# Causal attention in chunks of query blocks i and 7-i instead of 512 neighbouring queries, with one clip a step

## What is computed

```
Q = concatenate([Qc, Qr], axis=-1)          # (4, 16, 2048, 24)
K = concatenate([Kc, Kr], axis=-1)
scores = clip(einsum('bhqd,bhkd->bhqk', Q, K), -80.0, 80.0)
scores = where(causal, scores, -inf)
weights = softmax(scores / sqrt(24), axis=-1)
attn = einsum('bhqk,bhkd->bhqd', weights, V)
return attn.transpose(0, 2, 1, 3).reshape(B, S, 256) @ W_O
```

## Time and profile before

| | |
|---|---|
| runs | 2262.58, 2269.71, 2274.1 us; median 2269.71 us |
| profiled execution | 2265.95 us, of which the span is 2264.2 us |
| attention stage in the span | about 1093 to 2178 us |
| busy over the span | PE 2013.3 us (89%), DVE 1710.7 (76%), ACT 1582.6 (70%), POOL 829.8 (37%) |
| instructions | 45005 |
| instruction fetches by DMA | queue q8 149 packets, 2.44 MB; queue q14 53 packets, 0.43 MB |
| granted TensorE clock, mean | 0.968 |

### The profile page before, as it was taken

One profiled execution on the slowest core, in us unless ns is written; L12 is line 12 of the kernel. 1 busy time (PEld: TensorE's weight loads), 2 busy tenths in 40 slices (PEclk: granted clock), 3 DMA queues, 4 the chain that ended last, 5 costly groups with the idle time before them and its releaser, 6 DMA issues. The chain is left out here.

```text
span 2264.2 us, 45005 instructions
## 1 busy us (share of the span) xinstructions
PE 2013.3 (89%) x18726; PEld 906.9 (40%) x18726; DVE 1710.7 (76%) x2493; ACT 1582.6 (70%) x1833; POOL 829.8 (37%) x653
## 2 busy tenths in 40 slices
PE   5999999999995878788799989989999989999985
PEld 2656556556563554555222222222222222222243
DVE  7866676675748899998577788777788777788874
ACT  5545455464544554555799999989999989999951
POOL 1645445455365666766111111111111111111135
PEclk9999999999996999989899999999999999999997
DMA  3001001001112555547421233330333330233337
GB/s 97 19 19 32 26 20 38 19 20 38 48 38 84 164 159 153 168 130 195 116 49 41 68 76 72 75 71 20 76 76 76 71 74 16 67 76 81 112 103 261
DMA packets 118090, 178.00 MB, mean 79 GB/s; under 512 B 7424, under 2 KB 93184, under 8 KB 114048
## 3 DMA queue, kind: packets, MB, share of 16 engines
q1 hardware_dynamic: 115856, 172.89, 28.3%
q10 hardware_dynamic: 2032, 2.24, 0.3%
HBM read 91.21 MB, written 83.89 MB: 77 GB/s over the span
## 5 line engine op out<-in xcount | busy, mean ns | idle before, releaser
L1647 DVE TENSOR_SCALAR c_probs<-c_probs 128x512 f32<-128x512 f32 x1088 | 744.7, 723 | 181.0 <-ACT c_probs L1617 157.9
L1617 ACT ACTIVATE c_probs<-c_ps_b 128x1536 f32<-128x1536 f32 x544 | 852.8, 1568 | 0.0
L1703 PE MATMUL c_ps_o<-c_probs,c_v 128*32 128x512 f32 (+3 forms) x5120 | 583.3, 541 | 26.3 <-POOL c_probs L1662 22.4
L1662 POOL TENSOR_SCALAR_AFFINE_SELECT c_probs<-c_probs 128x512 f32<-128x512 f32 x256 | 192.5, 771 | 897.3 <-DVE c_probs L1647 897.3
L1681 PE MATMUL c_ps_a<-c_qk 24*128 24x512 f16 (+3 forms) x1920 | 445.1, 344 | 60.8 <-ACT c_probs L1616 41.0
L1681 PE MATMUL c_ps_b<-c_qk 24*128 24x512 f16 (+3 forms) x5760 | 456.3, 348 | 8.6 <-issue 8.6
L1616 ACT ACTIVATE c_probs<-c_ps_a 128x512 f32<-128x512 f32 x544 | 384.4, 707 | 77.7 <-PE c_ps_b L1681 39.5
L1681 PEld LDWEIGHTS c_ps_a<-c_qk 24*128 24x128 f16 x1920 | 144.4, 92 | 524.3 <-ACT c_probs L1617 351.1
L258 POOL TENSOR_TENSOR a_hidh<-a_hid,a_hidh 128x512 f16<-128x512 f32 x128 | 169.0, 1338 | 234.9 <-ACT a_hidh L356 231.0
L1703 PEld LDWEIGHTS c_ps_o<-c_probs,c_v 128*32 128x32 f32 x5120 | 112.2, 109 | 278.5 <-DVE c_probs L1647 126.2
L667 PE MATMUL a_ps<-a_xnh,a_w 128*128 128x512 f16 x768 | 172.0, 379 | 12.0 <-ACT a_hid L351 12.0
(11 more groups left out here) (242 smaller groups left out, 2913.7 us busy)
## 6 DMA issues: line engine op xcount, KB each, us to landing
c_qk<-qk_d SPq DMA_DIRECT2D x64, 384.0 KB
v_d<-b_val SPq DMA_DIRECT2D x16, 1024.0 KB
c_v<-v_d SPq DMA_DIRECT2D x16, 1024.0 KB
attn_d<-c_onorm SPq DMA_DIRECT2D x64, 256.0 KB, 3.1
rows<-in_x SPq DMA_DIRECT2D x16, 512.0 KB, 4.9
x_d<-rows_out SPq DMA_DIRECT2D x16, 512.0 KB, 3.2
rows<-x_d SPq DMA_DIRECT2D x16, 512.0 KB, 5.0
qk_d<-b_qc SPq DMA_DIRECT2D x64, 128.0 KB
```

Of the source, the lines that this page charges most:

```text
L1617: nc.scalar.activation(probs[:, t % NPROB, PARTS[1]], ps_b[:, t % 2], ACT.Exp, scale=unscale).then_inc(exp_b_done, 1)
L1647: nc.vector.tensor_scalar(tile, tile, P_MAX, P_MIN, ALU.min, ALU.max).then_inc(clip_done, 1)
L1662: pool.affine_select(out=tile, in_=tile, compare_op=ALU.is_ge, fill=0.0, base=0, pattern=[[0, GH], [1, P]], channel_multiplier=-1).then_in ...
L1703: mm = nc.tensor.matmul(ps_o[j * VW:(j + 1) * VW, first_query:first_query + w], v[:, kt, j * VW:(j + 1) * VW], probs[:, step % NPROB, j, a ...
```

## The change

A chunk is now query blocks c and 7 - c of 256 queries, placed side by side in the 512 columns, so that each chunk has 8.5 steps. A group has 34 steps as before, and the stage 544. Chunk c has these steps:

- 2c + 1 steps with one key tile for all 512 columns, the last of them with a diagonal tile ("both");
- one `tail` of 384 + 128 columns with two diagonal tiles; its first piece crosses from one query block to the other, so that `scores` splits it in 128 + 256;
- steps of two pieces of 256 columns, both of the high block and with different key tiles ("pairs"): 6, 4, 2 and 0 of them for c = 0 to 3, the first with one diagonal tile;
- half of a step that it shares with its neighbour, in the place of D2.

Over a group that is 16 "both" steps, 4 tails, 12 pairs and 2 shared ones. The masked steps are spread over the chunk: in chunk 0 the order is both with mask, pair, tail, pair, pair, pair with mask, pair, pair, and then the shared step. The number of masks stays 16 in a group. The queries of a "both" step are read in two runs of 256, and a chunk is stored in two runs of 1 KB a row instead of one of 2 KB.

VectorE clips a step in one instruction over 2048 columns, which waits for the exp of heads 1 to 3. Only in the step in which it also moves out a chunk are there two: the clip of head 0, the transpose, and the clip of heads 1 to 3.

```diff
+    def chunk_steps(c):
+        high = HALVES - 1 - c
+        both = [[(c, kt, 0, CH, 0)] for kt in range(TPH * c + 1)]
+        tail = [(c, TPH * c + 1, 0, CH - P, P), (c, TPH * high + 1, CH - P, P, CH - P)]
+        units = [TPH * high] + list(range(TPH * (c + 1), TPH * high))
+        left = units.pop()
+        pairs = [[(c, units[i], 0, HALF, HALF), (c, units[i + 1], HALF, HALF, HALF)] for i in range(0, len(units), 2)]
+        plain = both[:-1] + pairs[1:]
+        masked = [both[-1], tail] + pairs[:1]
+        steps = [(plain if c else masked).pop(0)]
+        parts = len(masked) + 1
+        for i in range(parts):
+            steps += plain[len(plain) * i // parts:len(plain) * (i + 1) // parts] + masked[i:i + 1]
+        return steps, left
...
     def consumed(t):
-        return t + 2 if steps[t][2] == D2 else t + 1
+        return t + 2 if joined(t) else t + 1
...
+    def split_clip(t):
+        return t - LAG + 1 in end_at
...
-                    rows = d["attn"][g * GH:(g + 1) * GH, :, b * SEQ + c * CH:b * SEQ + (c + 1) * CH].rearrange("e r t -> (e r) t")
-                    sp.dma_start(rows, o_norm[:, e % OUTS, :]).then_inc(stored[e % OUTS], 16)
+                    rows = d["attn"][g * GH:(g + 1) * GH, :, b * SEQ:(b + 1) * SEQ].rearrange("e r (n t) -> (e r) n t", t=HALF)
+                    sp.dma_start(rows[:, c::HALVES - 1 - 2 * c][:, 0:2], o_norm[:, e % OUTS, :].rearrange("p (n t) -> p n t", t=HALF)).then_inc(stored[e % OUTS], 16)
...
                 for t in range(N + LAG + 3):
-                    for after, task in ((-1, to_tokens), (0, reciprocal), (1, normalise), (2, to_channels)):
+                    for after, task in ((0, reciprocal), (1, normalise), (2, to_channels)):
                         if t - LAG - after in end_at:
                             task(end_at[t - LAG - after])
+                    if t < N and split_clip(t):
+                        clip(t, PARTS[0])
+                    if t - LAG + 1 in end_at:
+                        to_tokens(end_at[t - LAG + 1])
                     if t < N:
-                        clip(t)
+                        clip(t, PARTS[1] if split_clip(t) else slice(0, GH))
...
-                    for c, kt, at, w, first_query in pieces(t):
-                        for i, (hk, hq) in enumerate(TERMS):
-                            for j in range(GH):
...
+                    for c, kt, at, w, column in steps[t]:
+                        for x, n, tokens in queries(q, c, column, w):
+                            for i, (hk, hq) in enumerate(TERMS):
+                                for j in range(GH):
+                                    rows = slice(VW * j, VW * j + D_QK)
+                                    into = ps_b[:, t % 2, j - 1, at + x:at + x + n] if j else ps_a[:, 0, at + x:at + x + n]
+                                    mm = nc.tensor.matmul(into, k[rows, hk, kt * P:(kt + 1) * P], tokens[rows, hq],
+                                                          start=(i == 0), stop=(i == len(TERMS) - 1), tile_position=(VW * j, 0))
```

More of the change, by code:

```diff
@@ L1489, in attention @@
 def attention(nc, d, rows_out, score_scale, first, ahead):
[L1491 to L1505, removed]
+    HALF = CH // 2
+    HALVES = SEQ // HALF
+    TPH = HALF // P
     LAG = 3
@@ L1511, in attention, with query_tile @@
     PARTS = (slice(0, 1), slice(1, GH))
[L1512 to L1521, removed]
+    def query_tile(c, column):
+        block, inside = (c, column) if column < HALF else (HALVES - 1 - c, column - HALF)
+        return block * TPH + inside // P
@@ L1523, in products, with joined @@
+    steps, group_of = [], []
+    for g in range(BATCH * GROUPS):
+        for c in range(0, CPB, 2):
+            (one, left), (two, right) = chunk_steps(c), chunk_steps(c + 1)
+            steps += one + [[(c, left, 0, HALF, HALF), (c + 1, right, HALF, HALF, HALF)]] + two
+        group_of += [g] * (len(steps) - len(group_of))
+    N = len(steps)
+    def joined(t):
+        return len({piece[0] for piece in steps[t]}) == 2
     def products(t):
-        now = pieces(t)[:1] if steps[t][2] == D2 else pieces(t)
@@ L1526, in products @@
-        if t and steps[t - 1][2] == D2:
-            return [(t,) + p for p in now] + [(t - 1,) + pieces(t - 1)[1]]
+        now = steps[t][:1] if joined(t) else steps[t]
+        if t and joined(t - 1):
+            return [(t,) + p for p in now] + [(t - 1,) + steps[t - 1][1]]
         return [(t,) + p for p in now]
-    ordered = [(steps[t][0], p[1], t) for t in range(N) for p in products(t)]
     chunks = BATCH * GROUPS * CPB
     end_of = {}
-    for g, c, t in ordered:
-        end_of[g * CPB + c] = t
+    for t in range(N):
+        for p in products(t):
+            end_of[group_of[t] * CPB + p[1]] = t
@@ L1539, in consumed @@
     def consumed(t):
-        return t + 2 if steps[t][2] == D2 else t + 1
-    diagonals = {FULL: (), D0: (0,), D13: (0, CH - P), D2: (0, HALF)}
+        return t + 2 if joined(t) else t + 1
+    diagonals = [[at + x for c, kt, at, w, column in p for x in range(0, w, P) if query_tile(c, column + x) == kt] for p in steps]
     masks = [0]
     for t in range(N):
-        masks.append(masks[-1] + len(diagonals[steps[t][2]]))
+        masks.append(masks[-1] + len(diagonals[t]))
+    def split_clip(t):
+        return t - LAG + 1 in end_at
+    clips = [0]
+    for t in range(N):
+        clips.append(clips[-1] + (2 if split_clip(t) else 1))
     with ExitStack() as ctx:
@@ L1658, in _ @@
                 for t in range(N):
-                    for at in diagonals[steps[t][2]]:
-                        pool.wait_ge(clip_done, 2 * t + 2)
+                    for at in diagonals[t]:
+                        pool.wait_ge(clip_done, clips[t + 1])
                         tile = probs[:, t % NPROB, :, at:at + P]
@@ L1666, in _, with queries @@
             def _(pe):
+                def queries(q, c, column, w):
+                    tokens = q.rearrange("r h (n t) -> r h n t", t=HALF)
+                    if w == CH:
+                        return [(0, CH, tokens[:, :, c::HALVES - 1 - 2 * c][:, :, 0:2])]
+                    out, at = [], 0
+                    while at < w:
+                        x = column + at
+                        n = min(w - at, HALF - x % HALF)
+                        out.append((at, n, tokens[:, :, c if x < HALF else HALVES - 1 - c, x % HALF:x % HALF + n]))
+                        at += n
+                    return out
                 def scores(t):
-                    g = steps[t][0]
+                    g = group_of[t]
                     q, k = slots[g % 2].q, slots[g % 2].k
-                    if t == 0 or steps[t - 1][0] != g:
+                    if t == 0 or group_of[t - 1] != g:
                         pe.wait_ge(slots[g % 2].loaded, 16 * Operands.LOADS * (g // 2 + 1))
@@ L1693, in values @@
                     else:
-                        pe.wait_ge(clip_done, 2 * t + 2)
-                    for step, c, kt, at, w, first_query in products(t):
+                        pe.wait_ge(clip_done, clips[t + 1])
+                    todo = products(t)
+                    for i, (step, c, kt, at, w, column) in enumerate(todo):
                         e = g * CPB + c
@@ L1698, in values @@
                         if opens:
+                            assert w == CH
                             opened.append(t)
@@ L1702, in values @@
                         for j in range(GH):
-                            mm = nc.tensor.matmul(ps_o[j * VW:(j + 1) * VW, first_query:first_query + w], v[:, kt, j * VW:(j + 1) * VW],
-                                                  probs[:, step % NPROB, j, at:at + w], start=opens, stop=(t == ends[e]),
+                            mm = nc.tensor.matmul(ps_o[j * VW:(j + 1) * VW, column:column + w], v[:, kt, j * VW:(j + 1) * VW],
+                                                  probs[:, step % NPROB, j, at:at + w], start=opens, stop=(t == ends[e] and i == len(todo) - 1),
                                                   tile_position=(0, j * VW))
```

9 lines of the change are left out of this document (4 added, 5 removed).

## The result

The changed kernel takes 2324.5 us (median of four runs, 2321.7 to 2327.6) beside 2269.3 for the kernel before; the ratio is 1.0246, interval 1.0216 to 1.0276. The forecast was 2322. Both of its terms were off, by nearly the same amount in opposite directions, and the experiments tell them apart.

What follows compares the result with a forecast made beforehand. ScalarE's exps bound the attention stage, 1.81 to 1.83 us a step, plus its waits for TensorE. 2265.95 - 12.9 (step 5) + 68 (halts) = 2321, forecast as 2322 us; range 2254 to 2360, main case 2290 to 2358.

Steps and rivals of the forecast that it cites:

- The 32 waits behind the shared step: ScalarE waits for a place in the ring, two in a group; 38.2 us stay, at steps 12 and 29.
- Narrow matmuls: TensorE's narrower matmuls in pairs and tails keep the same columns a step, so they cost 0 us.
- Rival 3: TensorE becomes the bound of each pair and tail: +12 us on the main case, 2334 us; chance 0.08.
- The halts: TensorE runs out of instructions while a packet stands behind a group's loads; 36% more records, +68 us net.
- the mean halt: TensorE's halt behind a load averages 5.4 us, over 14 loads 76 us.
- the table's 7.8 to 10.5 us: TensorE's halts when the first blocked instruction request comes 1.8 to 0 us after the load's issue.
- r + C: Time from load issue to first blocked request, plus how long one packet's worth lasts; halt is 16.5 - r - C.
- the low clock: TensorE's granted clock falls after a halt, the next step waiting 1.18 us more; 11 us for 9 long halts.
- Rivals 1 and 2: Instruction fetch: rival 1, keeps up, 2251 to 2257 us, chance 0.14; rival 2, halts grow in proportion, +8 us, 0.13.
- Step 5 and the clips: At a group's start step 5's wait goes, -18.9 us, and 0.4 us a group comes back: net -12.9 us.
- the single clip's 0.3 us of lateness: VectorE's single clip ends 0.3 us later behind the exp, covered by two steps of 1.83 us before the products.
- Rival 4: VectorE falls behind at 64 chunk ends, 1.2 us each: +77 us in place of the gain; chance 0.02.

Runs made afterwards that it cites:

- the ring of five: Five places instead of four for the exps, loads in bursts: changed kernel with two clips a step 2202.4 us, kernel before 2210.1 us.
- two clips and bursts: Changed kernel with loads in three bursts and two clips in every step: 2245.0 us, where bursts with one clip took 2251.3.
- the old chunks with narrow pieces: Kernel before with 14 of 24 full steps of a group done as two pieces of 256 columns: 2329.3 us, ratio 1.0254.

## Why the prediction came out as it did

**The bound, and what stays.** ScalarE's floor, 1.83 us a step by the spacing of ends, is the same in all runs. The 32 waits behind the shared step stayed at 38.2 us, at steps 12 and 29, as forecast; that they were for a place in the ring is shown by the ring of five.

**Narrow matmuls: 0 us.** Right. With two clips and bursts every step of pairs, but for step 12 with its wait for the ring, takes 1.83 to 1.84 us in the median from end to end (step 4, which took 1.86 with one clip, too), and so do the narrow steps of the old chunks away from a load. Rival 3 falls.

**The halts: +68 forecast, +45 to +50 measured.** The mechanism was right: a halt behind each of the 14 loads, each ended by a late packet. Waits behind loads rose from 18.6 to 67.9 us, +49.3; taking the loads out gives +49.6 by the stages. By the medians it is (2324.5 - 2250.3) - (2273.7 - 2244.3) = +45, across two groups of runs. Two of the term's parts were mis-sized, in opposite directions.

The first is the mean halt, 5.4 us forecast and 3.06 measured; 14 x 2.3 is 33 us too much. The forecast let TensorE go on 16.5 us after every load's issue, from the two longest halts of before. It went on 12.4 to 17.5 us after it, 15.1 in the mean, and mostly early where the halt was long: five of the six longest halts ended 12.4 to 14.3 us after the issue, the longest, of 4.80 us, at 14.3. Nothing near the table's 7.8 to 10.5 us occurred. That fits a packet which came early when it was asked for early, but no trace shows the requests. The other 0.9 us of the mean is in r + C.

The second is the low clock, for which I took 11 us: ScalarE waited 67.9 us for halts of 42.8, 25 more. The extra time goes with the granted clock behind each halt. Three of the 14 halts (1.78, 2.22 and 0.89 us) have a granted clock of 1.00 in the 4 us behind them, and ScalarE's waits for them are 4.7 us for 4.9 of halts. The window behind the one of 2.22 us:

```profile
1695.05:1699.05 4.00, 4.00 (x74) 1.71 (x78) 1.25 (x2) 3.73 (x5) 0.46 (x1) 1.00 0.25 81
```

 The other eleven have 0.50 to 0.77, and there it waited 63.5 us for 37.9. Before it was 7.1 for 7.1 us in the seven halts with a full clock and 10.9 for 7.0 in the two without. The length of a halt is not what decides: of two in the old chunks with narrow pieces, one of 3.09 us had 1.00 behind it and cost ScalarE 3.12, one of 3.12 us had 0.59 and cost 4.41. A halt with a low clock behind it thus cost 2.3 us more than its length, where the forecast had 1.2.

The rule of the Trainium skill ("Runtime: NRT & Kernel Launch", instruction fetch mechanics) that TensorE has room for 2048 instructions would have made this term 0. The traces do not show that room in use, since TensorE halted 423 to 520 records behind a packet; whether it is smaller here or was not filled stays open. They agree with blocks of 16 KB (3.03 MB in 185 packets). Rivals 1 and 2 fall: the halts add up to 42.8 us, three times those of before, for 36% more records.

**Step 5 and the clips: -12.9 forecast, +4 to +6 measured.** This is the step of the prediction that failed. The wait at step 5 went, as forecast. At step 6, for which I had 0.4 us, 0.61 was left, and 0.41 came up at step 25, with smaller losses at steps 1 and 17: per group 1.37 us saved and 1.53 lost, by the spacing of ends. What failed is the sentence that the single clip's 0.3 us of lateness is covered by the two steps until the products. It is for a step without masks. For a step with two, the masks stand between: they start 0.27 us later behind the exp (1.33 us after its end and not 1.06), the second then starts just behind the next clip instead of just ahead of it, and the two took 2.26 us, not the 1.35 that they take beside two short clips. The forecast costed masks at 0.93 us each, and only at a group's start. The chunks by themselves are not at fault: with two clips, and loads in bursts, a median group is 0.85 us shorter than before. Rival 4 (VectorE behind at every chunk end, 1.2 us each) did not come; with two clips, the one wait left that lies behind VectorE's work at a chunk's end is the 0.41 us at step 25.

**Sum.** -12.9 + 68 = 55 forecast; +5 + 48, some 53 to 55 measured. The direction came from a mechanism that the runs bear out. That 2322 is so close is luck: two errors of nearly 20 us cancel.

## What to carry over

When a change splits matmuls without adding columns, count instructions against the packets in which they arrive: an engine's busy time will not show it, but a halt put down to "issue" in the middle of a step, behind a large load, does. Here the cure was in the loads: given out in bursts of at most 1 MB, they cost next to nothing. The cost of a halt is more than its length where the granted clock is low behind it. Look also for what a longer instruction does to its neighbours: fewer and longer clips saved VectorE time that nobody waited for, and slowed the masks that somebody did.

## What the runs showed that I had not expected

- Behind a load of 3 MB an instruction packet of 16 KB landed 9.5 to 14.8 us after the load's issue. When the same bytes came in small runs over 18 us of issues, or in bursts of at most 1 MB, hardly a halt was left.
- Two masks on GpSimd take 1.35 us beside two clips of VectorE and 2.26 beside one of 2048 columns, though the total of VectorE's work is less; which of mask and clip starts first, by less than 0.1 us, decided which of them got longer.
- Halts behind which the granted clock stayed 1.00 cost ScalarE their own length (4.7 us of waits for 4.9, before 7.1 for 7.1); those with 0.50 to 0.77 behind them cost 2.3 us more each (63.5 for 37.9).
